# GpSimd's hold during the second fp16 parts of x, taken away for batches 1 to 3

## What is computed

```python
Q, K, V = x @ wq.T + bq, x @ wk.T + bk, x @ wv.T + bv      # per head 32 wide
scores  = einsum('bhqd,bhkd->bhqk', Q, K) / sqrt(32)
scores  = where(causal, scores, -1e9) * head_gates[:, :, None, None]
out     = einsum('bhqk,bhkd->bhqd', softmax(scores), V)
x1      = layernorm(x + out @ wo.T + bo)
```

## Time and profile before

| | |
|---|---|
| median of 3 runs | 1771.5 us |
| lowest and highest run | 1766.73 and 1774.2 us |
| the profiled execution's own time | 1766.87 us |
| its span, first to last instruction | 1765.1 us |
| mean granted TensorE clock | 0.978 of full speed |
| busy PE, DVE, POOL, ACT | 1639.7, 1310.2, 1078.2, 1049.2 us |

### The profile page before, as it was taken

The page is one execution under the profiler, slowest core; times in us unless marked ns, Lnnn a source line. Parts: engine busy times, 40 slices in busy tenths (PEclk is TensorE's granted clock), DMA queues, the critical chain, the costliest instruction groups (busy, mean ns, idle before and its releaser), DMA issues. The chain is left out here.

```text
span 1765.1 us, 36425 instructions
## 1 busy us (share of the span) xinstructions
PE 1639.7 (93%) x13031; PEld 723.8 (41%) x13046; DVE 1310.2 (74%) x2947; ACT 1049.2 (59%) x1844; POOL 1078.2 (61%) x1020
## 2 busy tenths in 40 slices
PE   5998999999999999999897899999999997899997
PEld 2433443433433334333343444444444443444333
DVE  6778757787577875777935678888788776788798
ACT  6576655675556665567663366566575554555577
POOL 4077887678775787758713786777777775000044
PEclk9999999999999999999999999999999999899999
DMA  8312102231022310222235456556565341772375
GB/s 296 119 27 85 31 24 61 73 105 32 22 59 74 105 32 22 60 74 61 90 118 169 95 125 166 131 140 163 137 165 142 106 127 49 256 230 72 116 276 199
DMA packets 219613, 195.71 MB, mean 111 GB/s; under 512 B 118952, under 2 KB 169640, under 8 KB 218536
## 3 DMA queue, kind: packets, MB, share of 16 engines
q1 hardware_dynamic: 212904, 181.50, 36.0%
q10 hardware_dynamic: 6528, 11.88, 2.1%
HBM read 106.12 MB, written 38.14 MB: 82 GB/s over the span
## 5 line engine op out<-in xcount | busy, mean ns | idle before, releaser
L1189 DVE CUSTOM_DVE_ANT_0 a_mx<-a_mx,a_mqk 128x128 f32<-128x128 f32 (+3 forms) x512 | 242.2, 512 | 143.8 <-PE a_mx L1398 140.4
L998 ACT ACTIVATE a_P<-a_mx 128x512 f32<-128x512 f32 (+3 forms) x418 | 185.4, 494 | 137.6 <-PE a_mx L1416 83.5
L1412 PE MATMUL a_mx<-a_Qs,a_Ks 128*128 128x512 f16 (+3 forms) x768 | 228.7, 332 | 11.9 <-ACT a_P L998 3.9
L1398 PE MATMUL a_mx<-a_Ks,a_Qs 96*128 96x512 f16 (+3 forms) x768 | 225.2, 332 | 8.5 <-DVE a_nm L1189 4.1
L1272 POOL TENSOR_TENSOR a_P<-a_P 128x512 f32<-128x512 f32 (+3 forms) x164 | 159.6, 1002 | 85.1 <-PE a_o L1428 75.4
L998 ACT ACTIVATE share<-a_mx 128x512 f32<-128x512 f32 (+3 forms) x302 | 135.7, 493 | 99.6 <-PE a_mx L1416 55.8
L1272 POOL TENSOR_TENSOR a_P<-a_P,share 128x512 f32<-128x512 f32 (+3 forms) x192 | 178.0, 958 | 24.3 <-ACT share L998 18.9
L2358 PE MATMUL r_pj<-r_xT,share 128*128 128x512 f16 x768 | 186.1, 382 | 4.1 <-DVE r_AD L2222 2.4
L1192 DVE TENSOR_REDUCE a_nm<-a_mx 128x1 f32<-128x512 f32 x256 | 164.4, 682 | 30.3 <-PE a_mx L1398 29.4
L2358 PE MATMUL r_pj<-share,cth 128*128 128x512 f16 x672 | 167.9, 391 | 7.9 <-PEq L123 2.3
L3119 PE MATMUL f_pj<-f_xqT,f_wgu 128*128 128x512 bf16 x689 | 151.2, 379 | 1.5 <-DVE f_xqT L3003 0.8
(11 more groups left out here) (305 smaller groups left out, 3844.1 us busy)
## 6 DMA issues: line engine op xcount, KB each, us to landing
x_scratch<-rows SPq DMA_DIRECT2D x60, 256.0 KB, 2.9
rows<-x_scratch SPq DMA_DIRECT2D x56, 256.0 KB, 3.5
lead<-in_ctxT SPq DMA_DIRECT2D x38, 256.0 KB, 3.0
lead<-in_xT SPq DMA_DIRECT2D x18, 512.0 KB, 4.8
h_scratch<-f_h SPq DMA_DIRECT2D x3, 2816.0 KB, 8.5
f_h<-h_scratch SPq DMA_DIRECT2D x3, 2816.0 KB, 10.6
a_Ks<-a_kph SPq DMA_DIRECT2D x256, 32.0 KB, 1.9
a_Qs<-a_qph SPq DMA_DIRECT2D x256, 32.0 KB, 1.9
```

The source lines that it names most:

```text
L998: act.activation(Pf[pf.at[key]][:, off:512], pb[:, off:512], ACT.Exp).then_inc(p_exp, 1)
L1189: dve.tensor_tensor_reduce(bank_of(it)[:, 0:n], bank_of(it)[:, 0:n], mqk[:, 512 - n:512], 1.0, -3e38, ALU.add, ALU.max, nm[:, col:col + 1] ...
L1398: pe.matmul(pb[:, 0:n], Qs[s][0:96, j, qt * P:(qt + 1) * P], Ks[s][0:96, j, hf * 512:hf * 512 + n], start=True, stop=True).then_inc(max_mm, 1)
L1412: m = pe.matmul(pb[:, off:512], Ks[s][:, j, kt * P:(kt + 1) * P], Qs[s][:, j, qb * 512 + off:(qb + 1) * 512], start=True, stop=not diag)
```

## The change

The planner gets a second list, `shared`. A VectorE step whose kind is in `alone` records itself (and so holds GpSimd) only if its kind and batch are not in `shared`, which lists splitx of the batches 1 to 3. So for those twelve steps `until` is not set, GpSimd steps may be planned beside them, nothing is written into `yields`, and gpsimd() emits no wait on them. The hold for batch 0's splitx and for nwlo stays. No computing instruction is added or taken out, but everything that the planner places after the first splitx of batch 1 may get another place in the order.

```diff
@@ -134,7 +134,7 @@
-        self.alone, self.last, self.until, self.yields = (), None, 0.0, {}
+        self.alone, self.shared, self.last, self.until, self.yields = (), (), None, 0.0, {}
@@ -151,7 +151,7 @@
-        if engine == "DVE" and item[0] in self.alone:
+        if engine == "DVE" and item[0] in self.alone and item[:2] not in self.shared:
             self.last, self.until = item, self.now + length
         elif engine == "POOL" and self.last:
             self.yields[item], self.last = self.last, None
@@ -220,6 +220,7 @@
     flow = Flow()
     flow.alone = ("splitx", "nwlo")
+    flow.shared = [("splitx", b) for b in range(1, B)]
```

## The result

The changed kernel takes 1789.43 us (median of 6 runs, 1785.56 to 1791.24), the kernel before 1770.69 (6 runs, 1766.73 to 1774.2). The ratio is 1.0104, 95% interval 1.0087 to 1.0122. It is 19 us slower, beyond the 0.5% of the prediction and outside its range of 1764 to 1781 us. The profiled execution has a span of 1786.9 us.

A forecast was written before the change was run, and what follows sets the result against it. It took TensorE as the bound between the split stages and VectorE in them; -1.2 (GpSimd) + 1.6 (VectorE) + 0 (order) + 0 (clock) = +0.4 us on the 1771.5 us median gave 1772 us, range 1764 to 1781 us.

The forecast's parts named there:

- What bounds the kernel: Attention stage: TensorE bounds between the split stages, VectorE is fullest in the three short split stages, GpSimd bounds nowhere.
- -1.2 us for GpSimd's time: GpSimd gains 5.3 us in the split stages; only TensorE's own 1.2 us of waits for it reaches the end.
- VectorE's term: All twelve splits meet a running add and lose 0.575 us each, 2.3 us more than now; +1.6 us reaches TensorE.
- Rival 1: GpSimd keeps the interface over several adds while VectorE's splits wait: +13.9 us, 1785 us; chance 0.08.
- The order: New planned order on all engines from 162 us on: taken as 0, with 8.1 us to either side.
- The clock: TensorE's two low-clock stretches near the second and third split stages: taken as 0, at most +3.4 or -6.8 us.
- Rival 2: The new order is worse, with a third low-clock stretch: +11.9 us, 1783 us; chance 0.06 for more than 8.9 us.
- Rival 3: GpSimd's freedom and a better order reach TensorE, both low-clock stretches gone: -11.1 us, 1760 us; chance 0.09.
- Rival 4: GpSimd loses its time inside its adds instead, VectorE loses as before, order hardly moves: 0, 1771.5 us; chance 0.20.
- the forecast of 0.57: Whole kernel: a sum within a few us of +0.4 us, given a chance of 0.57.
- the missing idle time on GpSimd: Sign in the profile after: no GpSimd idle time that ends with a split, instead adds of about 2 us.
- the mean of L1052: Sign: mean length of VectorE's split about 1.8 us, 1.60 before; above 2.4 rival 1 is right.

The follow-up runs named there:

- attn_waits_off: Kernel before, attention stage alone, its order kept, but GpSimd no longer waits for the splits of batches 1 to 3: 972.99 us.
- attn_long_gap: As attn_waits_off, plus one GpSimd memset of 128x400 before the first add of key block 5 in units 5 and 9: 962.48 us.
- attn_late_hold_both: Kernel before, attention alone, with the holds for the first and second splits of batches 2 and 3 four adds later in GpSimd's order: 968.26 us.
- attn_changed_gap: Changed kernel, attention alone, with the two GpSimd memsets of attn_long_gap in front of the same adds: 972.86 us.
- attn_before: Kernel before, attention stage alone (retention and FFN left out, last four blocks of x1 without layer norm): 960.57 us.
- attn_after: Changed kernel, attention stage alone (retention and FFN left out, last four blocks of x1 without layer norm): 979.84 us.

## Why the prediction was wrong, point by point

**What bounds the kernel.** Right: TensorE between the stages, VectorE in them, GpSimd nowhere. The -1.2 us for GpSimd's time failed too: the waits for GpSimd did not go, they grew. In the changed kernel they are 3.2 us in 162 to 300 (2.1 of ScalarE, 1.1 of TensorE) where the earlier trace rows has 1.3, 1.9 in 380 to 500 and 1.4 in 610 to 730.

**VectorE's term (+1.6 us): the step that failed.** I let all twelve splits lose 0.575 us and set the upper bound at 1.64 each, from the split at 599.81. That row was read wrongly. It lost 1.64 us not because it met two adds, but because after the second add GpSimd stood at the hold: the 1.64 was the length of the queue up to the wait, and the change takes the wait away. The bound should have been the backlog: with 12 adds queued behind the running one that is 8.8 us, for the splits that meet a backlog, and nothing for those that don't. It came out as 2 splits x 7.2 us more (10.07 against 2.86 in attention alone), and the other ten hardly changed: 1.51 us on average against 1.45. The share that reaches the end, which I took as 0.7, is 11.9 / 14.4 = 0.83 in attn_waits_off, 10.5 / 16.4 = 0.64 from attn_long_gap to attn_waits_off, and 7.2 / 7.0, all of it, in attn_late_hold_both. That 0.7 lies among them is luck: it came from two stages, and the second stage, which I left out, has 1.7 us of waiting in its splits and 0.5 us of TensorE's waits on the maxima, less than the first.

**Rival 1** named the mechanism with a chance of 0.08 and the evidence for it, and asked for a mean loss above 1.2 us. The measured mean over the twelve is 35.2 / 12 - 1.22 = 1.7 us (35.2 us is the sum of the changed kernel's twelve), so the condition was met, by two splits. The chance was too low because I held the split at 379.64, which got in between two adds, against it. That win was the exception. In 12 profiled executions the first splits of batches 2 and 3 started with 0.8 us of the same add left, and 23 of these 24 lost the first boundary; without the hold the loser has no floor. The rival's 1785 us lie near the measured 1789 by luck: its 13.9 us are twelve splits that lose 1.64 each, where two lost 8.8 and the order did the rest. The rule of the Trainium skill that I weighed ("SBUF — State Buffer", section "Who interferes with whom"), that the loser blocks until the one instruction that was first is through, does not cover this: the loser stayed out for twelve further instructions.

**The order (0 us, 8.1 either way): the second step that failed.** It costs 12 to 13 us by the medians (11.8 and 12.9), 7.5 by the last reduces of attn_changed_gap's profiled execution. I took the scatter between two batches with the same order as the measure of what another order may do. That scatter says what noise does to one order, not what it is to stand in front of the wrong instruction. The price was to be had from rows: the reciprocal is five VectorE steps, 3.1 us (171.88 to 175.01 in the changed kernel, and 170.56 to 173.69 in the trace of before), and the last split and the last reduce of the maxima each release the next work of TensorE. An exchange with such a step would have been priced at 3 us per batch, 9 in all, and as a loss, since TensorE waits for both.

**The clock** was right at 0 as far as the mean shows: 0.976 against 0.978. The low stretches changed: they begin 4 us into each long split and are 10.2 us long (0.50 in 390.26 to 400.50 and in 618.95 to 629.19), and for a good half of that TensorE is idle anyway. The first stage now has one (0.88 in its window), but so has attn_before with the old order (0.50 in 165.21 to 168.62), so it is not shown to come from the change.

**Rival 2**, the new order worse, had a chance of 0.06 and came true in the sign: the order is 7 to 12 us of the loss. Its sum of 11.9 us meets that by luck, since 3.4 of it were for a third low stretch and its 8.1 for scatter. **Rival 3**, faster, finds nothing for it: the waits for GpSimd grew, and neither low stretch went.

**Rival 4**, that nothing would change, and the forecast of 0.57 both fall. Of the signs that I had listed, the missing idle time on GpSimd came true, the mean of L1052 came out at 2.9 us, above the 2.4 set for rival 1, the maxima of the first stage did come in another order, and the stretches between the stages were not the place: from the last split of one batch to the first of the next it is 208.2 and 206.7 us, against 204.9 and 207.6, and the loss is in the stages and in the unit behind them.

## What to carry to other kernels

A hold that keeps one engine off a shared port does two things: it costs its owner idle time, and it bounds what the other one can lose; before it is removed, the price to work out is the whole queue behind it, not one instruction. If the owner may run on, a single instruction that does not read SBUF, 0.4 us long, in front of the contended step gave VectorE its turn without any wait between the engines, though no faster than the hold (962.48 us against 961.1). When a planner's input changes, look at what moves in front of the two or three instructions that the bounding engine waits for, and price these exchanges, rather than calling the new order zero. And where a rule and a trace row disagree, as the split at 599.81 did here, find out what ended that row before it is used as a bound.

## What the runs showed of the hardware

- A VectorE instruction with two SBUF inputs that loses the port to GpSimd's adds can stay out for twelve of them back to back: 10.06 us instead of 1.22, with the adds at full speed. It happened at both places in each profiled execution of the changed kernel (whole twice, attention alone once) and of attn_waits_off (8 of 8).
- It ends where GpSimd has nothing to issue: 2.86, 3.80 and 6.38 us for a wait one, two and five adds further on.
- Not every split loses. With 0.8 us left of the same 512-column add, 23 of 24 first splits of batches 2 and 3 lost the first boundary, in 12 profiled executions; 379.64 in the kernel before won. With a 0.1 us memset between, one won and one lost; with 0.43 us all four won (two each in attn_long_gap and attn_changed_gap).
- In the four profiled executions without holds or memsets (the changed kernel twice, attn_after, attn_waits_off) the twelve splits that lost, the first of each batch, started when GpSimd had been at work for 20 us or more with no idle time; those of batch 1 took 2.4 to 2.8 us and began where GpSimd waited for ScalarE. The 21 others that met a running add with another behind it won at its end, all within 8 us of GpSimd's last idle time, and the next GpSimd instruction took a microsecond more, as here:

```profile
408.06 1.30 DVE L1052 SCALAR_TENSOR_TENSOR share<-lead,share 128x1024 f16<-128x1024 f32 x1
```

```profile
407.54 2.40 POOL L1273 TENSOR_TENSOR a_P<-a_P 128x256 f32<-128x256 f32 x2
```

What was left of the running add does not part them (0.8 us at 385.95, lost; 0.8 us at 400.31 in attn_waits_off, won). No run varied the time since GpSimd's last idle stretch, so that it decides is a guess, and the lone win at 379.64 speaks against it. Why a lost boundary is followed by lost ones alone stays open.
- VectorE counts as busy while it waits so. Its busy share can't tell this; the longest duration in a group can.
